# A two-layer cross-attention and ternary-FFN block on one core: rounding by a scaled 16-bit conversion, one-instruction normalisations and scales on GpSimd, 1024-column ScalarE instructions, new orders

## The reference

```python
def bit_linear(x, w, b):                       # stage 2, three times
    gamma_x = jnp.clip(jnp.max(jnp.abs(x), axis=-1, keepdims=True), 1e-05, None)
    scale_x = 127.0 / gamma_x
    x_dq = jnp.clip(jnp.round(x * scale_x), -128.0, 127.0) / scale_x
    gamma_w = jnp.clip(jnp.mean(jnp.abs(w)), 1e-05, None)
    w_dq = jnp.clip(jnp.round(w / gamma_w), -1.0, 1.0) * gamma_w
    return jnp.einsum('bsd,hd->bsh', x_dq, w_dq) + b

x = x + xattn8(_layernorm(x), ctx)             # stage 1 "A": 8 heads of 8 channels over 256 positions, rotary
x = x + out(silu(gate(xn)) * val(xn))          # stage 2 "B": xn = _layernorm(x), bit_linear, hidden 1024
x = x + masked_attention(_layernorm(x), ctx)   # stage 3 "D": 64 rows against 64 memory rows
x = x + proj(rms_norm(silu(g(x)) * u(x)))      # stage 4 "C": ternary weights per group of 64, hidden 1024
```

## Time and profile before

| what | value |
|---|---|
| median of three runs | 828.62 us (824.5 to 832.47) |
| span of the profiled execution | 828.8 us |
| TensorE busy | 759.6 us (92%) |
| VectorE busy | 739.1 us (89%) |
| ScalarE busy | 699.6 us (84%) |
| GpSimd busy | 636.2 us (77%) |

### The profile page before, as it was taken

How to read it: one execution, slowest core, us unless ns; L and a number is a source line. 1 busy time by engine, 2 the same in 40 slices (tenths; PEclk the granted TensorE clock), 3 DMA queues, 4 the chain that set the end, 5 groups by cost and what they waited for, 6 DMA issues and landing times. The chain is left out here.

```text
span 828.8 us, 22129 instructions
## 1 busy us (share of the span) xinstructions
PE 759.6 (92%) x6898; PEld 397.6 (48%) x6898; DVE 739.1 (89%) x1636; ACT 699.6 (84%) x1447; POOL 636.2 (77%) x1139
## 2 busy tenths in 40 slices
PE   2588999999999999999999999999999999998876
PEld 1233344444455554555555555555554545444444
DVE  3898798999999999999999999999999999987765
ACT  3788987988899898999898989999998888887644
POOL 3765656778898888988888888888888887777632
PEclk9555898999999999999999999999999999999999
DMA  8410222344434444544445444444444445434230
GB/s 287 140 54 19 71 67 64 76 105 94 112 87 108 109 110 110 108 116 112 104 111 116 112 101 110 109 105 106 117 101 120 99 91 115 95 87 91 57 72 20
DMA packets 197952, 82.59 MB, mean 100 GB/s; under 512 B 139710, under 2 KB 196670, under 8 KB 197836
## 3 DMA queue, kind: packets, MB, share of 16 engines
q1 hardware_dynamic: 193260, 74.63, 38.5%
q10 hardware_dynamic: 4576, 6.55, 2.4%
HBM read 28.15 MB, written 4.69 MB: 40 GB/s over the span
## 5 line engine op out<-in xcount | busy, mean ns | idle before, releaser
L1141 DVE TENSOR_REDUCE mx<-psS 128x2 f32<-128x512 f32 x512 | 334.1, 680 | 21.8 <-PE psS L630 20.2
L813 ACT ACTIVATE prob<-psT 128x512 f32<-128x512 f32 x512 | 292.5, 604 | 27.0 <-PE psT L638 21.6
L630 PE MATMUL psS<-KQ 31*128 31x256 f16 x1024 | 137.6, 285 | 7.0 <-DVE mx L1141 3.6
L652 PE MATMUL psW<-prob,vst 128*32 128x256 f32 x2048 | 143.0, 400 | 0.1
L741 PE MATMUL psW<-guT,xT 128*128 128x512 bf16 x512 | 132.6, 387 | 6.2 <-DMA xT<-stage 5.3
L638 PE MATMUL psT<-KQ 32*128 32x256 f16 x1024 | 130.4, 280 | 4.0 <-ACT prob L813 3.1
L652 PEld LDWEIGHTS psW<-prob,vst 128*32 128x32 f32 x2048 | 55.0, 112 | 61.4 <-issue 34.6
L741 PEld LDWEIGHTS psW<-guT,xT 128*128 128x128 f16 x512 | 43.1, 99 | 71.5 <-issue 36.5
L1025 POOL TENSOR_TENSOR hqB<-wide,rnd 128x512 bf16<-128x512 f32 x60 | 63.1, 1056 | 13.6 <-ACT wide L863 13.4
L1039 POOL TENSOR_TENSOR stage<-stage 128x512 f16<-128x512 f32 x60 | 69.7, 1162 | 2.5 <-ACT stage L924 1.8
L630 PEld LDWEIGHTS psS<-KQ 31*128 31x128 f16 x1024 | 40.4, 93 | 64.2 <-DVE mx L1141 38.0
(11 more groups left out here) (191 smaller groups left out, 1779.1 us busy)
## 6 DMA issues: line engine op xcount, KB each, us to landing
KQ<-hl SPq DMA_DIRECT2D x192, 64.0 KB, 1.9
xP<-in_x SPq DMA_DIRECT2D x32, 128.0 KB, 2.3
cP<-in_ctx SPq DMA_DIRECT2D x32, 128.0 KB, 2.1
xA<-in_x SPq DMA_DIRECT2D x32, 128.0 KB, 2.7
cB<-in_ctx SPq DMA_DIRECT2D x32, 128.0 KB, 2.3
oV<-uA SPq DMA_DIRECT2D x32, 128.0 KB, 2.1
out<-x SPq DMA_DIRECT2D x32, 128.0 KB, 2.0
oR<-rden_d SPq DMA_DIRECT2D x120, 32.0 KB
```

The costliest lines, as they stand in the source:

```text
L630: m = nc.tensor.matmul(psS[:, n % 2, T * k:T * k + T], KQ[p % DEEP][r, 1, g, 128 * k:128 * k + 128], KQ[p % DEEP][r, 0, g, :], start=True, ...
L652: m = nc.tensor.matmul(bank[32 * j:32 * j + 32, :], vst[p % DEEP][:, k, 4 * n + j, :], prob[:, (4 * n + j) % 8, k, :], start=(k == 0), sto ...
L813: m = nc.scalar.activation(flat(prob[:, n % 8, :, :]), psT[:, n % 2, :], ACT.Exp, scale=float(HC) ** -0.5)
L1141: m = nc.vector.tensor_reduce(mx[:, p % 2, :, 4 * (n % 4) + n // 4], psS[:, n % 2, :].rearrange("p (c s) -> p c s", c=NK), AX.X, ALU.max)
```

## The change

- The rounding to whole numbers is done by the conversion to fp16: the value is scaled so that one step of the quantisation is 2^-24, the spacing of the smallest fp16 numbers. `xr` goes, `xq` is one ScalarE instruction from xnB to fp16; `hr` is one ScalarE instruction of 1024 columns straight to the fp16 `hqB`, and `hq` goes. The scales carry the factor 2^24 back. The ternary weights of stage B are fp16 too.
- `sxB` and `sx` move from VectorE to GpSimd, with a power of -1 in place of the reciprocal.
- `xnB`, `xnD`, `xnC` on GpSimd are one tensor_scalar with two per-row scalars each. `ms` goes from four instructions to two.
- `sq` and `hh` are one instruction of 1024 columns each.
- All lists of steps (`HEAD`, `ORDER`, `TAIL`) are new.

```diff
+SUB = 16777216.0
 ORDER = {
-    "pe": """ro:-5 pv0:-1 T6:-1 S8:0 T7:-1 bg0:-3 S9:0 proj0:2 Bg0:-3 S10:0 T8:-1 T9:-1 S11:0 pv1:-1 Bd:-4 bv0:-3
...
+    "pe": """pT:-7 T5:-3 S7:-2 Cd1:-9 S8:-2 ro:-7 T6:-3 T7:-3 S9:-2 proj0:0 pv0:-3 T8:-3 bg0:-5 S10:-2 T9:-3 S11:-2 Bg0:-5 pv1:-3
...
-        tern = [sb(f"tern{i}", [P, 2 * HID], BF16) for i in range(3)]
+        tern = [sb(f"tern{i}", [P, 2 * HID], F16) for i in range(3)]
...
-                elif kind == "xr":
+                elif kind == "xq":
                     after(act, "sxB", p)
-                    after(act, "xq", p - 1)
-                    m = nc.scalar.activation(xrB[:], xnB[:], ACT.Copy, scale=sB[:, p % 2, 2:3], bias=ROUND)
-                elif kind == "xq":
-                    after(act, "xr", p)
                     after_late(act, p - 1, "lq", "qT")
-                    m = nc.scalar.activation(xqB[:, 0:T], xrB[:], ACT.Copy, bias=-ROUND)
+                    m = nc.scalar.activation(xqB[:, 0:T], xnB[:], ACT.Copy, scale=sB[:, p % 2, 2:3])
...
                 elif kind == "hr":
                     after(act, "sx", p)
-                    after(act, "hq", p - 1, n)
-                    m = nc.scalar.activation(hrB[:, 512 * n:512 * n + 512], hB[:, 512 * n:512 * n + 512], ACT.Copy,
-                                             scale=sB[:, p % 2, 8:9], bias=ROUND)
+                    after_late(act, p - 1, "lh", "ht", part=1)
+                    m = nc.scalar.activation(hqB[:], hB, ACT.Copy, scale=sB[:, p % 2, 8:9])
...
                 elif kind == "sq":
-                    after(act, "hC", p, n)
+                    after(act, "hC", p, 1)
                     after(act, "ms", p - 1)
-                    m = nc.scalar.activation(sqC[:, n, :], hC[:, n, :], ACT.Square, accum_out=ssq[:, n:n + 1])
+                    m = nc.scalar.activation(flat(sqC), flat(hC), ACT.Square, accum_out=ssq[:])
                 elif kind == "hh":
-                    after(act, "hC", p, n)
+                    after(act, "hC", p, 1)
                     after_late(act, p - 1, "lz", "hT", part=1)
-                    m = nc.scalar.copy(hhl[:, 0, n, :], hC[:, n, :])
+                    m = nc.scalar.copy(flat(hhl[:, 0, :, :]), flat(hC))
...
-                    inner(1, nc.gpsimd.tensor_tensor(centre[:], src[:], mv[:, 0:1].broadcast_to([P, T]),
-                                                     ALU.subtract))
                     after(pool, last_use, p - 1, part)
                     if kind == "xnC":
                         after(pool, "xl", p - 1)
-                    m = nc.gpsimd.tensor_tensor(dst[:], centre[:], rs[:, 1:2].broadcast_to([P, T]), ALU.mult)
+                    m = nc.gpsimd.tensor_scalar(dst[:], src[:], mv[:, 0:1], rs[:, 1:2], ALU.subtract, ALU.mult)
+                elif kind == "sxB":
...
+                    inner(1, nc.gpsimd.tensor_scalar(sc[:, 1:2], sc[:, 0:1], 1e-5, SUB / 127.0, ALU.max, ALU.mult))
+                    nc.gpsimd.tensor_scalar(sc[:, 4:5], sc[:, 1:2], gam_q[:, 0:1], None, ALU.mult)
+                    nc.gpsimd.tensor_scalar(sc[:, 5:6], sc[:, 1:2], sc[:, 1:2], gam_q[:, 1:2], ALU.mult, ALU.mult)
+                    m = nc.gpsimd.tensor_tensor(sc[:, 2:3], sc[:, 1:2], mone[:], ALU.pow)
+                elif kind == "sx":
...
+                    inner(1, nc.gpsimd.tensor_scalar(sc[:, 6:7], sc[:, 3:4], sc[:, 5:6], 1e-5, ALU.mult, ALU.max))
+                    inner(2, nc.gpsimd.tensor_tensor(sc[:, 7:8], sc[:, 6:7], mone[:], ALU.pow))
+                    nc.gpsimd.tensor_scalar(sc[:, 9:10], sc[:, 6:7], gam_q[:, 2:3], None, ALU.mult)
+                    m = nc.gpsimd.tensor_scalar(sc[:, 8:9], sc[:, 7:8], sc[:, 5:6], 127.0 / SUB, ALU.mult, ALU.mult)
...
-                elif kind == "hq":
-                    h = slice(512 * n, 512 * n + 512)
-                    after(pool, "hr", p, n)
-                    after_dma(pool, "ht", p - 1)
-                    m = nc.gpsimd.tensor_tensor(hqB[:, h], hrB[:, h], rnd[:].broadcast_to([P, 512]), ALU.subtract)
...
-                    inner(1, nc.gpsimd.tensor_tensor(sc[:, 0:1], ssq[:, 0:1], ssq[:, 1:2], ALU.add))
-                    inner(2, nc.gpsimd.tensor_tensor(sc[:, 1:2], sc[:, 0:1], eps[:, 1:2], ALU.mult))
-                    inner(3, nc.gpsimd.tensor_tensor(sc[:, 3:4], sc[:, 1:2], hsc[:, 2:3], ALU.add))
-                    m = nc.gpsimd.tensor_tensor(sc[:, 2:3], sc[:, 3:4], mhalf[:], ALU.pow)
+                    inner(1, nc.gpsimd.tensor_scalar(sc[:, 0:1], ssq[:], 1.0 / HID, hsc[:, 2:3], ALU.mult, ALU.add))
+                    m = nc.gpsimd.tensor_tensor(sc[:, 1:2], sc[:, 0:1], mhalf[:], ALU.pow)
...
-                elif kind == "sxB":
-                    after(dve, "amB", p)
...
-                elif kind == "sx":
-                    sc = sB[:, p % 2, :]
-                    after(dve, "amH", p)
```

More of the change, by code:

```diff
@@ new lines @@
+    "act": """E1:-2 hr:-5 vst:0 E2:-2 pD:-6 E3:-2 xq:-4 E4:-2 pTc:-6 E5:-2 xnP:1 hh:-7 E6:-2 E7:-2 hi:0 E8:-2 tB0:-4 E9:-2 u0:-2
+           E10:-2 xh:-6 E11:-2 E12:-2 tB1:-4 x1:-3 E13:-2 E14:-2 sq:-7 mxc:-1 E15:-2 md:-1 pc:1 th0:-6 th1:-6 u1:-2
+           E0:-1 xcTc:-5""",
+    "pool": """xb:-4 ms:-8 xnD:-6 rsB:-4 xnB:-4 sx:-5 r2:0 sxB:-4 rq:-4 rsP:1 rs:-6 rot:0 lo:0 rsC:-6 xnC:-6 om:-3 xl:-6 hl0:-7
+           hl1:-7 rsD:-5""",
+    "sp": """ov:-4 d1:-4 qT:-5 xP:1 or:-4 kq:-1 xT:-7 st:-9 cB:-6 hT:-8 sg:-3 cP:1 ht:-5 xA:-3""",
@@ L408, in build @@
         stB, mvB, rsB = sb("stB", [P, 6]), sb("mvB", [P, 2]), sb("rsB", [P, 2])
-        xnB, xrB = sb("xnB", [P, T]), sb("xrB", [P, T])
-        xqB, xqT = sb("xqB", [P, T + P], BF16), sb("xqT", [P, NK + 1, P], BF16)
+        xnB = sb("xnB", [P, T])
+        xqB, xqT = sb("xqB", [P, T + P], F16), sb("xqT", [P, NK + 1, P], F16)
+        xrb, xrbT = xqB[:, T:T + P].bitcast(BF16), xqT[:, NK, :].bitcast(BF16)
         rd = sb("rd", [P, 1])
         sB = sb("sB", [P, 2, 10])
-        wide = sb("wide", [P, 3 * HID])
-        aB, hrB, hB = (wide[:, HID * i:HID * i + HID] for i in range(3))
-        late = [tq[:, 1:3, :].rearrange("p a b -> p (a b)").bitcast(F32), wide[:, 0:2 * HID]]
+        wide = sb("wide", [P, 2 * HID])
+        aB, hB = (wide[:, HID * i:HID * i + HID] for i in range(2))
+        late = [tq[:, 1:3, :].rearrange("p a b -> p (a b)").bitcast(F32), wide[:]]
         tB = stage[:, 2, HID:2 * HID]
-        hqB, hqT = sb("hqB", [P, HID], BF16), sb("hqT", [P, 8, P], BF16)
+        hqB, hqT = sb("hqB", [P, HID], F16), sb("hqT", [P, 8, P], F16)
         x1b, x2 = sb("x1b", [P, 2, T]), sb("x2", [P, T])
@@ L698, in _ @@
                     r = slice(32 * (2 * (kind == "bv") + n), 32 * (2 * (kind == "bv") + n) + 6)
-                    m = nc.tensor.matmul(bank, xqT[r, NK, :], brow[r, :], start=True, stop=False)
+                    m = nc.tensor.matmul(bank, xrbT[r, :], brow[r, :], start=True, stop=False)
                 elif kind in ("Bg", "Bv"):
@@ L1269, in _ @@
                     after(dve, "aC", p, n)
[L1270 to L1271 removed]
+                    after(dve, "sq", p - 1)
+                    after(dve, "hh", p - 1)
                     after(dve, "hl", p - 1, n)
```

464 lines of the change are left out of this document (222 added, 242 removed).

## The result

The changed kernel takes 865.24 us (860.63 to 865.63) against 828.05 us of the kernel before in the same session. The two medians stand as 1.045 to 1; the ratio on record is 1.0415, 95% interval 1.0355 to 1.0475. Slower by 4%, and outside my range of 811 to 852 us.

The account below looks back on a forecast made before the run. TensorE and VectorE, nearly full, bound the kernel at 22.2 us a pair; afterwards TensorE alone, 22.0 us work plus 0.3 waits, 22.3. Over about 27 pairs +3 us, the end even: 831 us, range 811 to 852 us.

Parts of the forecast that it names:

- the +1.1 forecast: TensorE's work per pair: four more runs add 1.28 us, the old run of seven gives 0.2 us back.
- The 0.32 us of a run: TensorE: a run of S and T steps costs about 0.32 us whatever is in it, if no row group repeats.
- The case of 803 us: Faster rival, 8%: extra runs cost nothing, TensorE's work stays at 20.9 us, a pair takes 21.3 us.
- I leave 0.3 us of waits: TensorE, steady part: of 0.6 us idle and 1.3 us waits per pair, 0.3 us stays, mostly for transfers.
- 20.9 us as TensorE's own work: TensorE before the change, per pair: taken near the middle of the bounds 20.3 and 21.6 us.
- The sign I took for it: Weight loads of S and T waiting for mx and E, 1.3 us per pair, perhaps inside TensorE's busy time.
- I had 20.0 us a pair: VectorE: losing sx and sxB, together 1.3 us, takes it from 21.3 to 20.0 us per pair.
- The term for 1024 columns: ScalarE: an instruction of 1024 columns should take 1.18 us, from the slope between 256 and 512 columns.
- I take 0.45: GpSimd: each of three remaining normalising instructions takes 0.45 us, so normalising costs 2.3 us less per pair.
- Even within 1 us: The end, from 700 us on: savings and slower GpSimd scale steps in the last pairs' chains cancel within 1 us.
- Under 282 row maxima: Sign of being wrong, 300 to 700 us: with waits for xqT or hqT, the way through GpSimd is the new bound.
- Slower, TensorE as the only bound: Rival, 35%: work 22.0 us, idle 0.6 us unchanged, 0.2 us for sx and sxB: 22.8 us a pair, 847 us.

Follow-up runs that it names:

- e3: Kernel before with four full-array steps in TensorE's loop moved earlier, so 12 runs a pair for 8: 852.49 us, 1.0306.
- e6: Kernel before with only the GpSimd normalisations as one instruction: 825.14 us, 0.9979.
- e9: Changed kernel with sx and sxB back on VectorE, everything else as changed: 866.66 us, 1.0476.
- e7: Kernel before with only the rounding by conversion, hr in two halves, sx and sxB on VectorE: 820.43 us, 0.992.
- e10: e7 with sq and hh at 1024 columns, the short ms, and hl0 beside hl1: 835.04 us, 1.0102.
- e8: e7 with sx and sxB on GpSimd: 871.92 us, 1.054.
- e12: e7 with hr as one instruction of 1024 columns: 824.11 us, 0.9949.

## Why the prediction was wrong

**Right: who bounds, and, with some luck, the added work.** TensorE became the only bound, with mx and E waiting for it. Its busy time rose by 1.08 us a pair against the +1.1 forecast, its work by 1.0 to 1.4. The 0.32 us of a run from the earlier trace rows held for one to four steps. Two errors stood against each other here: I left out the 0.1 us on the step ahead of a run, so four runs cost 1.7 us (e3) and not 1.28, and what the dissolved long runs gave back was more than 0.2 us (before, the run of seven took 0.61 us and that of five 0.87, with whatever waiting was in them). "Changing tiling mode (not just tile) drains the TensorE" (the Trainium skill, TensorEngine Tiling (Array Packing), "Key Properties") is what the rows look like: the price lies on both sides of a run and hardly depends on what is in it. The case of 803 us, in which runs cost nothing, is ruled out by e3.

**The step that failed: "I leave 0.3 us of waits".** I took 20.9 us as TensorE's own work and the 1.3 us up to the period as waits that VectorE's and ScalarE's slack would end, all but 0.3. The start was near: by the shortest intervals it is 20.8 us of work and 1.3 of waiting. But after the change 0.8 us of waiting is still there, beside 22.2 of work where I had 22.0 (by the shortest whole pair, which counts more as work, the waiting goes from 0.8 to 0.6). The period rose by 0.87 us where I had 0.1, and about two thirds of the difference is waiting that did not go away. Over the 27 pairs of my sum the 0.77 us between them are 21 of the 34 us that I missed; the tail and the 4.6 us between profile and median are most of the rest.

It was an assumption, that an engine with slack answers at once. The sign I took for it, is idle time of the weight loads under open matmuls, and is no measure of what TensorE loses: it fell from 1.3 to 0.8 us a pair, while the weight loads' waits for KQ rose from 0.2 to 0.7. A possible reason, which no run shows: S n waits for mx n-2 through two psS places, and what mx stands behind in VectorE's list is not shortened by slack at the end of the pair.

**VectorE was relieved as forecast, and its busy time hides it.** I had 20.0 us a pair, it is 20.9: the busy time falls by 0.35 us, not 1.3. Yet the eight small steps were worth what I had. In the same 11 pairs, before and after, the instructions that read or write sB keep VectorE busy for the third number of each line (the count behind it):

```profile
313.06:556.72 243.66, 37.59 (x121) 1.00 0.48 109
318.07:571.34 253.27, 23.02 (x33) 1.00 0.45 105
```

That is (37.59 - 23.02) / 11 = 1.32 us. The durations of all of VectorE's instructions add up to 24.9 us a pair before and 23.5 after, 1.35 less. But instructions that follow each other without a pause overlap in the records by 0.08 us on average: 44 of 49 a pair did before, 32 of 41 do after. An engine that begins to wait loses this overlap, so its busy time falls by less than its work, or rises: in e3, with VectorE's list and code unchanged, it goes from 21.28 to 21.54 us.

**ScalarE.** The term for 1024 columns was 1.18 us and measured 1.156: right. The busy time of the pair falls by 0.5 us instead of 1.1, with the same effect as on VectorE (the durations add up to 1.6 us less), and the relief is worth nothing beside TensorE.

**GpSimd.** "I take 0.45" for the normalisation, bounds 0.267 to 0.614. It is 1.22 us, twice the upper bound. The bound was bad: an old instruction does one operation with a broadcast operand, the new one does two. GpSimd rose by 0.45 us a pair instead of falling by 2. It cost no time: e6 has the time of the kernel before with it, and in e9 GpSimd is 2.7 us a pair lighter than in the changed kernel, with no gain:

```profile
323.47:575.82 252.35, 247.03 (x2336) 126.43 (x2332) 236.47 (x540) 218.04 (x431) 187.34 (x308) 1.00 0.46 105
```

**The tail.** "Even within 1 us" was wrong by 6.6 us, cause open.

**The signs.** VectorE at 90%, ScalarE at 85% and TensorE at 98% came as I wrote for being right, and GpSimd's 85% told of the dear normalisation. Under 282 row maxima came too, but without the waits for xqT or hqT that I had tied to it: they are 0.6 and 0.7 us in the stretch. So the count pointed to TensorE, not to the way through GpSimd.

**The rivals.** "Slower, TensorE as the only bound" at 35% was the case that came. Of its mechanism e3 shows the work, +1.1 and more; the plain idle time did not stay at 0.6 us but fell to 0.4, and e9 shows nothing of the 0.2 us for the way through sx and sxB. So its 22.8 us a pair came near the 23.02 in part by luck, and with 29.6 us in the span for its 18 it was too small by the tail and the 0.2 us a pair. I ranked it second only because I credited the slack of the other engines. Put against single costs in the old order, it adds up about: e7 -5.5 us, e10 over e7 +14.6, four runs (e3) +25: +34 against the 37 measured. That it comes so near is luck: e8's 50 us are left out on the word of e9, e12's few too, and e3's four runs dissolve no long ones. It is a sum over different orders, so it orders the costs and proves none of the changed kernel's.

## What to carry to other kernels

Where small row-group steps are woven between full-array steps, count the runs, not the steps: here each cost TensorE the same with one step or four in it, so a new order is to be judged first by that count. When the busiest engine gets more work, take its whole addition as lost time; its waits on neighbours with new slack don't go away by themselves (here at most 0.5 of 1.3 us did), and others take their place. Measure that waiting between the engine's own steps, not by the idle time of its weight loads, and a neighbour's relief by durations, not by busy time. And with hand-laid orders keep the one edit that pays (here the rounding) on the old order, and time each edit alone before all lists are laid out anew.

## What the runs showed of the hardware that was not expected

- A GpSimd tensor_scalar with two per-row scalars takes 1.22 us for 128x256 in f32; a tensor_tensor with one broadcast operand takes 0.614. Here two operations in one instruction cost as much as two instructions.
- Instructions of VectorE that follow each other without a pause overlap by 0.08 us on average in the records, those of ScalarE by 0.11.
- A run of one to four row-group steps of TensorE takes 0.317 to 0.336 us, and the full-array step ahead of it some 0.1 us more (0.97 for 0.87); e3 measures 0.43 us for one more run.
- One-column steps on GpSimd take 0.24 to 0.34 us (tensor_scalar) and 0.55 to 0.57 us (power), here L994 to L1006.
- ScalarE at 1024 columns takes 1.156 us with a per-row scale, 1.061 for the square, 1.035 for a plain cast.
